# Attention inner loops of a two-layer hybrid model: query blocks of 1024 columns in place of 512

## What is computed

```python
def reference(L0_attn_a_x, ...):             # x: 8 x 2048 x 1024
    x = x + _L0_attn_a_ref(_layernorm(x), ...)   # 16 heads of 64, full softmax      ("l0a")
    x = x + _L0_ffn_ref(_layernorm(x), ...)      # shared and 8 routed experts       ("moe")
    x = x + _L0_attn_b_ref(_layernorm(x), ...)   # 16 heads of 64, window + selected ("l0b")
    x = x + _L0_ffn_ref(_layernorm(x), ...)      #                                   ("moe")
    x = x + _L1_attn_a_ref(_layernorm(x), ...)   # 8 heads, keys of 128 + 32 rotary  ("l1a")
    x = x + _L1_ffn_ref(_layernorm(x), ...)      # soft mixture of 16 experts        ("smoe")
    x = x + _L1_attn_b_ref(_layernorm(x), ...)   # 16 heads of 64, causal            ("l1b")
    x = x + _L1_ffn_ref(_layernorm(x), ...)      #                                   ("smoe")

# the core of each attention
scores = jnp.einsum('bhqd,bhkd->bhqk', q, k) * scale     # l1b, l0b: masked
attn = jax.nn.softmax(scores, axis=-1)
out = jnp.einsum('bhqk,bhkd->bhqd', attn, v)
```

## Time and profile before

| | us |
|---|---|
| median of two runs | 20116.71 |
| the two runs | 20180.82, 20052.59 |
| the profiled execution | 20074.55 |
| its span on the slowest core (3) | 20073.0 |
| median span of cores 0 to 3, of cores 4 to 7 | 20038.0, 19848.0 |

### The profile page before, as it was taken

One profiled execution on the slowest core, in us unless ns is written; L12 is line 12 of the kernel. 1 busy time (PEld: TensorE's weight loads), 2 busy tenths in 40 slices (PEclk: granted clock), 3 DMA queues, 4 the chain that ended last, 5 costly groups with the idle time before them and its releaser, 6 DMA issues.

```text
span 20073.0 us, 151760 instructions; the slowest of 8 cores (19813.0 to 20073.0 us)
## 1 busy us (share of the span) xinstructions
PE 11606.7 (58%) x36168; PEld 3851.8 (19%) x36168; DVE 4185.4 (21%) x6389; ACT 3269.6 (16%) x4414; POOL 2305.6 (11%) x3041
## 2 busy tenths in 40 slices
PE   4555554888884444444458989666664344555433
PEld 1111010333331010101013333211110220111012
DVE  1111111222112232323222222211112212222230
ACT  2222222100001212121210101111111012111210
POOL 0000000433211000000023431100001110000011
PEclk6555555898775555555568999755555555555555
DMA  0000000222220000000012222100000110000002
GB/s 20 1 3 5 0 5 1 35 29 34 29 26 10 0 9 0 9 0 9 0 14 33 31 34 30 14 1 0 1 1 2 22 19 1 4 5 5 1 2 51
DMA packets 357118, 251.11 MB, mean 13 GB/s; under 512 B 46446, under 2 KB 314798, under 8 KB 354115
## 3 DMA queue, kind: packets, MB, share of 16 engines
q0 software_dynamic: 351712, 222.51, 8.4%
q1 hardware_dynamic: 4580, 18.90, 0.3%
HBM read 450.89 MB, written 8.39 MB: 23 GB/s over the span
## 4 chain that ended last, share of the span: by engine, by line
PE 55%; ACT 13%; DVE 13%; issue 9%; POOL 5%; DMA 3%; DVEq 1%; ACTq 1%; SPq 0%; POOLq 0%
PE mpa L759 7%; PE mpa L765 7%; PE mpr L800 7%; ACT apt L578 6%; PE aop L591 5%; PE asp L574 5%; PE bop L1097 3%; DVE S_row L597 2%; ACT lpt L1282 2%; PE lop L1286 1%; ACT bp L1061 1%; POOL S_yT L385 1%; PE lsp L1279 1%; PE lsp L1275 1%; ACT bp L1083 1%
## 5 line engine op out<-in xcount | busy, mean ns | idle before, releaser
L591 PE MATMUL aop<-apt,avv 128*65 128x512 bf16 x1664 | 1010.2, 607 | 1797.9 <-ACT apt L578 1397.2
L759 PE MATMUL mpa<-S_yT,mw 128*128 128x512 bf16 x6144 | 1596.7, 407 | 387.2 <-DMA mw<-moe_w12T 387.2
L578 ACT ACTIVATE apt<-asp,S_negb 128x512 bf16<-128x512 f32 x1664 | 1143.2, 687 | 3216.1 <-PE asp L574 3216.0
L765 PE MATMUL mpa<-S_yT,mw 128*128 128x512 bf16 x6144 | 1574.0, 403 | 0.0
L800 PE MATMUL mpr<-mxe,mw 128*128 128x512 bf16 x6144 | 1405.8, 394 | 62.1 <-POOL mxe L779 46.6
L1097 PE MATMUL bop<-bp,bv 128*65 128x512 bf16 x864 | 524.5, 607 | 1243.8 <-DVE bp L1065 762.4
L574 PE MATMUL asp<-aq,ak 64*128 64x512 bf16 x1664 | 1003.6, 603 | 12.5 <-DVE S_negb L446 9.1
L744 POOL DMA_DIRECT2D mw<-moe_w12T x1536 | 820.6, 597 | 684.0 <-PE mpa L759 657.5
L597 DVE RECIPROCAL S_row<-aop 1x512 f32<-1x512 f32 x128 | 429.0, 3352 | 2159.5 <-PE aop L591 2159.5
L759 PEld LDWEIGHTS mpa<-S_yT,mw 128*128 128x128 bf16 x6144 | 631.0, 103 | 1219.9 <-issue 776.1
L771 ACT ACTIVATE msil<-mpa 128x512 f32<-128x512 f32 x768 | 458.9, 597 | 2315.1 <-PE mpa L759 2076.3
(11 more groups left out here) (275 smaller groups left out, 11106.6 us busy)
## 6 DMA issues: line engine op xcount, KB each, us to landing
mw<-moe_w12T POOLq DMA_DIRECT2D x1536, 64.0 KB, 2.6
mw<-moe_w3T POOLq DMA_DIRECT2D x192, 256.0 KB, 8.3
sw<-sm_w POOLq DMA_DIRECT2D x256, 64.0 KB, 2.5
sw<-sm_w POOLq DMA_DIRECT2D x64, 256.0 KB, 4.6
S_xT<-xin SPq DMA_DIRECT2D x8, 1024.0 KB
xout<-S_xT SPq DMA_DIRECT2D x8, 1024.0 KB
awr<-l0a_wqkvT POOLq DMA_DIRECT2D x96, 64.0 KB, 2.5
bcos<-mask_band POOLq DMA_DIRECT2D x4, 544.0 KB, 4.0
```

Of the source, the lines that this page charges most:

```text
L578: ex = p.s(lambda e, b=b: e.activation(pt[b][:], sps[b][:], AF.Exp, bias=c.negb[:, 0:1]), wait=[mm, avd.get(idx - 2)])
L591: e.matmul(ops[:], va[kt][:, 65 * hh:65 * hh + 65], pt[b][:], start=(idx == 0), stop=(idx == nn - 1)),
L759: ents1 = [(lambda e, st, sp, i=i, sl=sl, b=b, co=co: e.matmul(pa1[b][:], wsl[i][:, co:co + 128], c.yT[i][:, sl], start=st, stop=sp), ([ld ...
L765: ents2 = [(lambda e, st, sp, i=i, sl=sl, b=b, co=co: e.matmul(pa2[b][:], wsl[i][:, co + 128:co + 256], c.yT[i][:, sl], start=st, stop=sp) ...
```

## The change

In all four attention stages a block has 1024 queries: two blocks in place of four. A matmul still writes 512 columns, so each one becomes two (`hf` 0 and 1), with the same weights and the two halves of the queries; the exponential, the mask product, the reciprocal, the copy and the last product become one instruction of 1024 columns. sps, pt, ops and rps are twice as wide; PSUM holds the two sps tiles (4 banks), one ops and one rps (2 each), so ops and rps are no longer doubled, and the first values' matmul of a block waits for the last product of the block before it (prev_ml). In l1a there is no room for rps: the spread of the reciprocal goes to sps[0], and the next block's first scores wait for the last product.

The tile lists are made for 1024 queries. In l1b a head has 8 + 16 wide tiles, 16 of them masked. In l0b a head has 8 + 13 band tiles and 4 + 12 below tiles, 4 of the latter without a mask; its mask tiles and their loads grow from 2176 and 2048 columns to 2688 and 2560. In emit_attn_std the p.barall() between the heads and the load of the output weights is gone.

The core of the diff (emit_attn_std; the other two functions are changed in the same way):

```diff
-                sps = [hses.enter_context(_pst(nc, f"asp{i}", [128, 512], F32))
+                sps = [hses.enter_context(_pst(nc, f"asp{i}", [128, 1024], F32))
                        for i in range(2)]
-                opsq = [hses.enter_context(_pst(nc, f"aop{i}", [65, 512], F32))
-                        for i in range(2)]
-                rpsq = [hses.enter_context(_pst(nc, f"arp{i}", [64, 512], F32))
-                        for i in range(2)]
+                ops = hses.enter_context(_pst(nc, "aop", [65, 1024], F32))
+                rps = hses.enter_context(_pst(nc, "arp", [64, 1024], F32))
...
-                    for qb in range(4):
+                    for qb in range(2):
+                        q0 = 1024 * qb
                         kts = [kt for kt in range(NT)
-                               if (not cfg["causal"]) or 128 * kt <= 512 * qb + 511]
+                               if (not cfg["causal"]) or 128 * kt <= q0 + 1023]
...
-                            mm = p.t(lambda e, kt=kt, b=b, ti=ti, ro=ro, qsl=qsl: e.matmul(
-                                sps[b][:], ka[ti][ro:ro + 64, 128 * kt:128 * (kt + 1)],
-                                qa[ti][ro:ro + 64, qsl], start=True, stop=True),
-                                wait=[expd.get(idx - 2)])
+                            for hf in range(2):
+                                mm = p.t(lambda e, kt=kt, b=b, ti=ti, ro=ro, q0=q0,
+                                         hf=hf: e.matmul(
+                                    sps[b][:, 512 * hf:512 * (hf + 1)],
+                                    ka[ti][ro:ro + 64, 128 * kt:128 * (kt + 1)],
+                                    qa[ti][ro:ro + 64,
+                                           q0 + 512 * hf:q0 + 512 * (hf + 1)],
+                                    start=True, stop=True),
+                                    wait=([expd.get(idx - 2)] if hf == 0 else None))
                             ex = p.s(lambda e, b=b: e.activation(
                                 pt[b][:], sps[b][:], AF.Exp, bias=c.negb[:, 0:1]),
                                 wait=[mm, avd.get(idx - 2)])
...
+                            for hf in range(2):
+                                av = p.t(lambda e, kt=kt, b=b, hh=hh, idx=idx, hf=hf,
+                                         nn=len(kts): e.matmul(
+                                    ops[:, 512 * hf:512 * (hf + 1)],
+                                    va[kt][:, 65 * hh:65 * hh + 65],
+                                    pt[b][:, 512 * hf:512 * (hf + 1)],
+                                    start=(idx == 0), stop=(idx == nn - 1)),
+                                    wait=(wv + [prev_ml] if (idx == 0 and hf == 0)
+                                          else wv))
...
-            p.barall()
             tok = None
             for i in range(2):
                 tok = p.dma(lambda e, i=i, g=g: e.dma_start(
```

In l0b the order of an iteration's matmuls is keys, selection for hf 0, then for hf 1. In l1a the closing part reads:

```diff
+                            rc = p.v(lambda e: e.reciprocal(c.row1[0:1, 0:1024],
+                                                            sm1[:]),
+                                     wait=[avd[NT - 1]])
+                            for hf in range(2):
+                                rp = p.t(lambda e, hf=hf: e.matmul(
+                                    sps[0][0:128, 512 * hf:512 * (hf + 1)],
+                                    c.ones_row[0:1, 0:128],
+                                    c.row1[0:1, 512 * hf:512 * (hf + 1)],
+                                    start=True, stop=True),
+                                    wait=([rc, expd.get(NT - 2)] if hf == 0 else None))
...
+                            prev_ml = ml
+                            expd = {-2: ml, -1: expd.get(NT - 1)}
```

More of the change, by code:

```diff
@@ L587, in emit_attn_std @@
                                 expd[idx] = dv
                                 wv = [dv]
[L589 to L594 removed]
+                            av = None
@@ L1095, in emit_l0b @@
-                            av = p.t(lambda e, kt=kt, b=b, h4=h4, idx=idx, ops=ops,
-                                     nn=len(tiles):
-                                     e.matmul(ops[:], va[kt][:, 65 * h4:65 * h4 + 65],
-                                              pt[b][:], start=(idx == 0),
-                                              stop=(idx == nn - 1)),
-                                     wait=(wv + [mld.get(jq - 2)] if idx == 0 else wv))
-                            avd[idx] = av
@@ new lines, in emit_l0b @@
+                            av = None
+                            for hf in range(2):
+                                av = p.t(lambda e, kt=kt, b=b, h4=h4, idx=idx, hf=hf,
+                                         nn=len(tiles): e.matmul(
+                                    ops[:, 512 * hf:512 * (hf + 1)],
+                                    va[kt][:, 65 * h4:65 * h4 + 65],
+                                    pt[b][:, 512 * hf:512 * (hf + 1)],
+                                    start=(idx == 0), stop=(idx == nn - 1)),
+                                    wait=(wv + [prev_ml] if (idx == 0 and hf == 0)
+                                          else wv))
@@ new lines, in emit_l0b @@
+                            avd[idx] = av
+                        expd = {-2: expd.get(len(tiles) - 2),
+                                -1: expd.get(len(tiles) - 1)}
+                        rc = p.v(lambda e: e.reciprocal(c.row1[0:1, 0:1024],
+                                                        ops[64:65, :]),
+                                 wait=[avd[len(tiles) - 1], prev_rp])
+                        rp = None
+                        for hf in range(2):
+                            rp = p.t(lambda e, hf=hf: e.matmul(
+                                rps[:, 512 * hf:512 * (hf + 1)],
+                                c.ones_row[0:1, 0:64],
+                                c.row1[0:1, 512 * hf:512 * (hf + 1)],
+                                start=True, stop=True),
+                                wait=([rc, prev_cp] if hf == 0 else None))
@@ new lines, in emit_l1a @@
+                                for hf in range(2):
+                                    p.t(lambda e, kt=kt, b=b, h2=h2, hf=hf: e.matmul(
+                                        ops[:, 512 * hf:512 * (hf + 1)],
+                                        va[kt][:, 128 * h2:128 * (h2 + 1)],
+                                        pt[b][:, 512 * hf:512 * (hf + 1)],
+                                        start=(kt == 0), stop=(kt == NT - 1)),
+                                        wait=([ex, prev_ml] if (kt == 0 and hf == 0)
+                                              else [ex]))
+                                    av = p.t(lambda e, kt=kt, b=b, hf=hf: e.matmul(
+                                        sm1[:, 512 * hf:512 * (hf + 1)],
+                                        c.ones_col_bf[:],
+                                        pt[b][:, 512 * hf:512 * (hf + 1)],
+                                        start=(kt == 0), stop=(kt == NT - 1)))
```

292 lines of the change are left out of this document (125 added, 167 removed).

## The result

| | before | after |
|---|---|---|
| median of the runs on one chip, us | 20,016.84 | 19,736.31 |
| their range, us | 19,836 to 20,246 | 19,605 to 19,789 |
| profiled execution, us | 20,074.55 | 19,665.85 |
| mean span of the 8 cores in it, us | 19,943 | 19,599 |

The changed kernel takes 0.9884 of the time (95% interval 0.9847 to 0.9921), 1.2% less. By the bound of 2% that is "same". The forecast was 19,820 us with a range of 19,640 to 20,050. In some executions one die is granted a lower clock than the other and the time is up to 3% longer; the times and ratios given with the experiments leave these out.

A forecast was written before the change was run, and what follows sets the result against it. Serial hand-overs between TensorE and ScalarE, with no engine full, were taken as the bound. Terms -426 + 24 + 312 + 4 - 166 + 37 + 10 - 42 = -247 us gave 19,820 us, 80% range 19,640 to 20,050.

The forecast's parts named there:

- The exponential: All attention stages: one exponential of 1024 columns takes 1125 ns, 0.44 us more than one of 512.
- The second rival: Wide exponentials pay for two PSUM banks: 0.25 us for each of 1744, +436 us, 20,260 us; chance 0.03.
- The added matmul: Second-half matmul in wide iterations: 0.427 us beside an equal shape, upper bound 0.535; 0.52 us in l1a.
- the first rival: Weight loads of second-half matmuls aren't hidden: 0.108 us for each of 3232, +349 us, 20,180 us; chance 0.08.
- its smaller form: Only the 65-column loads of the values' matmul are exposed: 1488 x 0.108 = +161 us, 19,990 us; chance 0.08.
- The mask product: Masked tiles of l1b and l0b: the product of 1024 columns costs 0.28 us more, bounds 0.2 and 0.43.
- Iterations: Wide iterations: l0a 3.42 us, l0b band 4.23, masked below 5.09, plain below 4.28, l1a 5.67.
- The masks in the range: Mask slope between its bounds: 912 wide masks x 0.1 us either way, part of the forecast's range.
- The barrier: Before the output projection: without p.barall() the weight load is issued at the group's start; 8 groups x 5.2, -42 us.
- the block ends: Two narrow ends equal one wide within half a us for 96 blocks; l1a's 16 blocks cost +37 us.
- the +4 for the mask loads: l0b: the longer mask loads add about 1 us in each group, +4 us.
- The chance for the clock: TensorE's clock rises in l1a for three quarters of it: -384 us, 19,440 us; chance 0.12.

The follow-up runs named there:

- the first experiment: The changed kernel run once more, unaltered, on another chip beside three variants: 19,566 us against 20,028 for the kernel before, ratio 0.976.
- scores ahead: Against the kernel before, 512 columns kept, scores issued two tiles ahead of the values on TensorE, block ends run beside the next block: 15,883 us, ratio 0.789.
- last kernel: Against the kernel with key-tile pairs and next scores issued early, scores in l0a and l1b contract over 128 rows, keys zero-padded: 14,617 us, ratio 0.731 to before.
- the same loop of pairs: Against the kernel before, one exponential covers two key tiles of a 512-query block, next pair's scores issued before this one's values: 15,098 us against 19,993.

## Why the prediction was right

The direction and the mechanism hold: two stages gain, one loses, one is even, and the barrier adds a little. The size is short by a third: the sum had -247 us where the parts measure -356. That the whole came out as near as 1.2% against the forecast 1.5% is partly luck, since the executions on that chip showed less than the parts. Point by point:

- **The exponential**: forecast 1125 ns, measured 1114. The second rival, that two banks cost as much as two instructions, has fallen.
- **The added matmul**: 0.43 us, also for the 65-column loads (two of them are what 3.41 us leaves over 2.125 and the exponential's 0.43). The loads of equal shapes are hidden, and the first rival has fallen with its smaller form.
- **The mask product** of 1024 columns: forecast 0.70, measured 0.69 us. The reciprocal: 6.55 and 6.55.
- **Iterations**: l0a 3.42 forecast, 3.41 measured; band 4.23 and 4.20; masked below 5.09 and 5.05; l1a 5.67 and 5.72.
- **The masks in the range**: the prediction counts 912 wide ones; there are 784 (256 in l1b, 528 in l0b). This touches only the width of the range, by 13 us.
- **The barrier**: -42 forecast, -49 measured; in l1b the gap had been larger (6.5 to 10.7 us with the barrier) than the one of l0a from which I took it.
- **The mis-sized term is the block ends.** I booked two narrow ends and one wide one as equal outside l1a, from an end in l0a. In l0b they aren't. Rows of the kernel before that show it:

```profile
6714.91 0.61 PE L1097 MATMUL bop<-bp,bv 128*65 128x512 bf16 x1 [1.51 <-DVE bp L1090]
...
6722.26 0.69 DVE L1118 TENSOR_TENSOR bo<-bop,S_srec 64x512 bf16<-64x512 f32 x1 [0.17 <-DVE S_srec L1113]
6723.12 0.43 DVE L1065 TENSOR_TENSOR bp<-bp,bcos 128x512 bf16<-128x512 bf16 x1 [0.17 <-DVE bo L1118]
6723.80 0.61 PE L1097 MATMUL bop<-bp,bv 128*65 128x512 bf16 x1 [2.03 <-DVE bp L1065]
```

The exponential of the new block's first tile ends at 6722.55, but its mask waits until 6723.12 for the product of the old block, on the same engine. From values to values are 8.89 us, 6.23 over a band iteration, not 5.54. The wide end, from values to values, is

```profile
6213.59 1.04 PE L1099 MATMUL bop<-bp,bv 128*65 128x512 bf16 x2 [2.21 <-DVE bp L1091]
...
6229.14 1.03 PE L1099 MATMUL bop<-bp,bv 128*65 128x512 bf16 x2 [2.94 <-DVE bp L1084]
```

15.55 us, 11.35 over its band iteration, against 2 x 6.23 = 12.46: 1.1 us saved for each of 32 pairs, -36. With the iterations a little shorter than booked (-16) this gives l0b's +266 in place of +312 (the +4 for the mask loads lies outside these stretches and wasn't measured). In l0a the narrow ends come to 7.9 us from exponential to exponential, two of them 0.3 us over the wide one; with the iteration 0.015 us under the booked one that makes most of the step from -426 to -445. In l1b the same two sources leave +4 in place of +24; I haven't separated them there. In l1a the iteration is 0.05 us longer than booked (+12), and the ends took that back and a little more: -132 against -127.
- **The chance for the clock**: the clock stayed at 0.50, as forecast with 0.88. The argument for that, a share of busy time that grows only to 75%, was weak: the changed kernel is busy 70% of l1a at 0.50, and with equal shapes side by side it is busy 65% at 0.61.
- **The sum**: -247 forecast; the stages and the barrier give -356 (-445, +4, +266, -132, -49). The ratios on two chips, 1.2% and 2.4% of 20,000 us, lie on both sides of it; the first experiment shows a spread that can do this. The forecast's own distance, some 110 us, is the sum of small steps with one sign, most of them at block ends.

## What to carry to other kernels

Widening an instruction on a serial chain saves its fixed cost once for each hand-over; count first which of the new columns are dead, and what of the old double buffers has to be given up for the room. Here the dead halves of one stage cost 532 us, more than the largest gain of another, and taking the second tile from the other operand's side avoids both. Where no engine is full, the order on the list can be worth more than the size of its items: scores ahead at the old width, with the block ends hidden too, gave some 4,200 us where the width gave 356, and in l1a the order of equal shapes gave 250 us where the width gave 132.

## What the runs showed of the hardware

- A weight load costs nothing behind a matmul of its own shape, with the same weights or others (0.38 to 0.43 us from start to start, 512 columns at the lower clock; shapes 128x128, 64x128, 128x65 and 128x1). It costs 0.09 to 0.14 us where the next matmul has 64 or 32 rows against 128, or one column against 128. Not every change of shape costs: 128x128 and 128x65 follow each other as fast as equal ones (last kernel: 0.43 us at the lower clock, 0.22 at the upper). With TensorE as the bound the exposed loads are 0.24 of a tile's 1.10 us.
- TensorE can be busy 306.54 of 309 us and be granted 0.50 of its clock. With 128 rows in place of 64 under half of its matmuls, and with that no exposed loads, the same loop of pairs is granted 0.84 instead of 0.50, and in l1a the order of the matmuls alone moved 0.50 to 0.61. The Trainium skill ("TensorE: Matmul & The Clock Gate", section "What's actually happening") has the throttle released by how busy TensorE is; in l0a of the narrow kernel with scores ahead that didn't happen in any of the four groups, nor in its l1a (busy 279.4 of 279.5 us, granted 0.50).
- In an expert stage the granted clock differs between cores of one execution (0.90 and 0.85), and their times for that stage by 170 us; over everything outside the heads the cores differ by 100 to 280 us. In such a program an edit of 50 us is read from its own stretch, not from the whole.
